# Splitting ScalarE's two-instruction pieces over two rows of the scans, in a Mamba layer with a mixture of experts

## The reference, cut to what matters

```python
xz = einsum('bld,ed->bel', h, in_proj_w);  x, z = xz[:, :1024], xz[:, 1024:]
x = silu(causal_conv4(x) + conv_b)
x_dbl = einsum('bdl,kd->blk', x, x_proj_w)        # dt_lo (32), B (16), C (16)
delta = softplus(dt_lo @ dt_proj_w.T + dt_proj_b)
for t:  hs = hs * exp(delta_t * A) + delta_t * B_t * x_t;   y_t = sum_n(hs * C_t)
y = (y + x * D) * silu(z)
x1 = layernorm(h + y @ out_proj_w.T)
# top 2 of 8 experts, softmax of the two logits
out = layernorm(x1 + sum_k w_k * (x1 @ expert_w[k].T + expert_b[k]))
```

## Time and profile before

| | |
|---|---|
| runs of the kernel | 2264.38, 2264.75 and 2259.15 us, median 2264.38 |
| the profiled execution | 2260.66 us, span 2258.9 us |
| mean granted clock of PE | 0.947 |
| busy over the span | PE 90%, DVE 88%, POOL 82%, ACT 73% |
| batches 2 to 6 | from 561.2 to 1865.3 us, 260.8 us each |

### The profile page before, as it was taken

How to read it: one execution, slowest core, us unless ns; L and a number is a source line. 1 busy time by engine, 2 the same in 40 slices (tenths; PEclk the granted TensorE clock), 3 DMA queues, 4 the chain that set the end, 5 groups by cost and what they waited for, 6 DMA issues and landing times. The chain is left out here.

```text
span 2258.9 us, 30428 instructions
## 1 busy us (share of the span) xinstructions
PE 2036.0 (90%) x8624; PEld 1200.9 (53%) x8624; DVE 1982.8 (88%) x2191; ACT 1658.4 (73%) x3074; POOL 1854.5 (82%) x1505
## 2 busy tenths in 40 slices
PE   8897779898999989999899998999899998879898
PEld 3444455455564555545555555645556455655453
DVE  5899989989999999899999999899998998989912
ACT  5767858767598866979588875988678886667534
POOL 2988999788998889889898889989898997696503
PEclk9897879989899999999999999999999999789999
DMA  5432142367754786557863678557855576495775
GB/s 164 160 108 70 40 148 77 95 212 229 246 126 124 231 289 180 137 171 233 280 172 106 209 249 264 118 153 248 293 150 136 176 245 236 146 272 189 246 270 117
DMA packets 222085, 412.79 MB, mean 183 GB/s; under 512 B 29880, under 2 KB 36152, under 8 KB 221920
## 3 DMA queue, kind: packets, MB, share of 16 engines
q1 hardware_dynamic: 180448, 322.36, 42.6%
q0 software_dynamic: 20496, 57.16, 12.4%
q10 hardware_dynamic: 20976, 31.33, 4.3%
HBM read 299.37 MB, written 85.72 MB: 170 GB/s over the span
## 5 line engine op out<-in xcount | busy, mean ns | idle before, releaser
L1784 ACT ACTIVATE dA<-delta,negA 128x512 f32<-128x512 f32 (+1 forms) x1146 | 714.4, 637 | 317.4 <-DVE hst L1976 250.1
L1925 POOL TENSOR_TENSOR hst<-u,Bbc 128x512 f32<-128x512 f32 x666 | 880.7, 1427 | 57.4 <-PE hTp L1334 36.3
L1976 DVE TENSOR_TENSOR_SCAN hst<-dA,hst 128x512 f32<-128x512 f32 x672 | 790.3, 1207 | 44.0 <-ACT dA L1784 36.8
L1334 PEld LDWEIGHTS hTp<-ident,hst 128*128 128x128 f32 x4096 | 496.2, 149 | 318.4 <-issue 172.2
L1334 PE MATMUL hTp<-ident,hst 128*128 128x128 f32 x4096 | 557.9, 288 | 96.5 <-DVE hst L1976 24.4
L1965 DVE SCALAR_TENSOR_TENSOR y<-hTp,Ct,y 128x1024 f32<-128x1024 f32 x463 | 585.1, 1264 | 54.5 <-PE hTp L1334 51.6
L1925 POOL TENSOR_TENSOR first_dbu<-u,Bbc 128x512 f32<-128x512 f32 x222 | 295.1, 1411 | 16.5 <-DVE hits L2057 11.6
L1976 DVE TENSOR_TENSOR_SCAN hst<-dA,first_dbu 128x512 f32<-128x512 f32 x224 | 263.2, 1207 | 17.7 <-issue 9.1
L1318 PE MATMUL bank<-wslot,hidT 128*128 128x512 f32 x512 | 250.3, 621 | 8.1 <-ACT zs L1666 6.2
L1318 PE MATMUL bank<-wslot,tokT 128*128 128x512 f32 x496 | 233.3, 598 | 4.0 <-ACT tokT L1686 3.9
L1318 PE MATMUL bank<-delta,tokT 128*128 128x512 f32 x480 | 224.4, 600 | 0.0
(11 more groups left out here) (187 smaller groups left out, 2886.7 us busy)
## 6 DMA issues: line engine op xcount, KB each, us to landing
wslot<-in_w_expT SPq DMA_DIRECT2D x90, 1024.0 KB
Bbc<-b_scratch SPq DMA_DIRECT2D x113, 256.0 KB
wslot<-in_w_inT SPq DMA_DIRECT2D x26, 1024.0 KB
y<-scaled POOLq DMA_DIRECT2D x49, 512.0 KB
zs<-sorted_tokens ACTq DMA_DIRECT2D x91, 256.0 KB, 6.1
sorted_results<-ysb SPq DMA_DIRECT2D x90, 256.0 KB
res<-in_w_expT SPq DMA_DIRECT2D x18, 1024.0 KB, 5.7
gate_scratch<-zs SPq DMA_DIRECT2D x64, 256.0 KB, 2.8
```

What stands on the lines that cost most here:

```text
L1334: mm = nc.tensor.transpose(hTp[q % 2][:, tok(j)], hst[n % 2][:, j, start:start + P], ident[:, :])
L1784: nc.scalar.activation(decay_of(step, halved), delta[w.odd][:, j, cols], ACT.Exp, scale=negA[:, j, n:n + 1]).then_inc(exp_done, 1)
L1925: nc.gpsimd.tensor_tensor(dbu_row(n, j), u[w.odd][:, j, :], Bbc[n % 2][:, :], ALU.mult).then_inc(dbu_done, 1)
L1976: nc.vector.tensor_tensor_scan(hst[n % 2][:, j, :], dA[j % 2][:, :], dbu_row(n, j), 0.0, ALU.mult, ALU.add).then_inc(scan_done, 1)
```

## The change

ACT's plan for batches 2 to 6 is rewritten after planning, while the other engines keep theirs. Every double piece is issued as two single ones, the second at the earliest in the next row, that is behind the next row's exponential. The order of the pieces is kept: what stood behind a double piece in the same row follows its second half into the next row. `Segment.single` then keeps `piece` from calling the second half itself. In numbers: of 149 ACT pieces in a batch 48 are doubles (8 each of z, z2, sig2, dt, dt2 and 4 each of ln1, ln2), and all 48 second halves move by one row. Along with them 18 other pieces move by one row: z2 of tiles 0, 5 and 7, x2, scale6, x6, sig and sig2 of group 5, scale7, sig and sig2 of group 7, skip 2, 4 and 6, the copies xsT2 and xsT3, dt2 of groups 2 and 4. No instruction is added or removed.

```diff
+def one_by_one(pieces, steps):
+
+    rows, last = [], 0
+    for row, x, _ in pieces:
+        for k, name in enumerate(SINGLE.get(x[0], (x[0],))):
+            last = min(max(row + k * (last <= row), last), steps - 1)
+            rows.append((last, (name,) + x[1:], 0))
+    return rows
...
         self.fine = any(x[0] in ("dt1", "rs1") for x in pieces)
+        self.single = self.fine or steps == STEPS
...
+        if self.single and not self.fine:
+            order["act"] = one_by_one(order["act"], steps)
...
                     nc.scalar.activation(a, a, ACT.Ln, bias=1.0).then_inc(sig_step, 1)
-                    if not w.seg.fine:
+                    if not w.seg.single:
                         piece(w, ("sig3", j))
```

## The result

| | before | after |
|---|---|---|
| runs | 2264.57 us median of 4 (2259.15 to 2268.25) | 2335.36 us median of 4 (2320.26 to 2340.14) |
| ratio | | 1.0303, 95% interval 1.0259 to 1.0346 |
| profiled execution | 2260.66 us, span 2258.9, clock 0.947 | 2320.26 us, span 2318.5, clock 0.936 |
| busy | PE 90%, DVE 88%, POOL 82%, ACT 73% | PE 89%, DVE 86%, POOL 80%, ACT 71% |
| batches 2 to 6 | 1304.1 us, 260.8 each | 1369.8 us, 274.0 each |

The change makes the kernel 3% slower, 7 us beyond the top of the range. The profiled execution, 2320.26 us, is the fastest of after and lies inside the range; of the others, at a granted clock of 0.928 to 0.934, only time and clock are on record.

A forecast was written before the change was run, and what follows sets the result against it. The prediction took PE and DVE, running almost without a break, to bound the kernel. Its terms summed to 9.8 us a batch, 49 us in five, giving 2310 us against the profiled 2260.66, with a range from 2273 to 2328.

The forecast's parts named there:

- (d): Rows 79 to 80: x6's copy goes behind exponential 80, sig3 and scale6, DVE's taps wait; 2.5 us a batch.
- (a): z0, row 39: exponential 40 comes ahead of z1 to z3, the yT copies come 1.25 later; 0.8 us a batch.
- (b): Rows 70 and 74: copies x0 and x2 each go behind an exponential and a third half; 0.7 us a batch.
- (c): Row 78: sig3 goes ahead of x5, behind an exponential for which ACT must idle; 0.6 us a batch.
- (f): skip3: exponential 95 comes later and dt3 goes in between, so PE's yinit3 is late; 0.9 us a batch.
- (h): moe4, dt_5 and yinit4 follow dt_4's moved halves; exponential 111 and the copies behind slip; 0.9 us a batch.
- the 0 net: Rows 46 and 53: earlier exponentials win at most 1.6 us a batch, taken as 0 net of delays behind them.
- (e): Row 82: sig7's last half is late, POOL's product and PE's xproj follow at +1.4; 1.0 us a batch.
- (g): Rows 99 to 100: copies xsT2 and xsT3 come later and PE's moe2 waits for them; 2.4 us a batch.
- rival of the clock: Row 82 and moe2: PE's clock falls more often, seven drops of 1.7 us, 12 us on top, 2322; chance 0.14.
- later waits absorb half: DVE's waits for ACT overlap with its lateness; 4.9 us a batch, 24 us, 2285; chance 0.17.
- faster: Rows 46, 53, 62, 66, 95: DVE's waits for dA go, halves stay hidden; 2.2 a batch, 2250 us; chance 0.11.

The follow-up runs named there:

- e7: The kernel before with only the eight norms a batch (ln1 and ln2) split; 2255.66 us, ratio 0.9994.
- e9: The kernel of e6 plus two extra 512-column matmuls ahead of x7 and wT's four small matmuls done twice; 2312.2 us, ratio 1.0243.
- e13: The kernel of e8, with each share of the x projection waiting for its own tile of x; ratio 1.0183.
- e14: The kernel of e9, with each share of the x projection waiting for its own tile of x; ratio 1.0177.
- e6: The kernel after, with PE turning token tile 3 seven times instead of once, right ahead of moe2; 2321.31 us, ratio 1.0273.
- e8: The kernel after, with x2, x6, scale6, scale7, skip2, skip4, skip6, xsT2 and xsT3 kept ahead of the exponential; 2309.55 us, ratio 1.023.
- e12: The kernel after, with each share of the x projection waiting for its own tile of x; ratio 1.0265.

## Why the prediction was wrong in size

The direction, the places and what starts the loss were right: halves moved behind exponentials that wait for scans, and what stands behind them is late by the exponential and the idle time. What two of the steps left out is how that lateness goes on, through POOL's line and through PE's clock. The terms against the rows:
- **(d) x6**: 2.5 foretold, 2.45 in the rows of every batch; the taps wait 2.59.
- **(a)**: 0.8 foretold, 0.8 lost at row 42. The place was another: PE did not wait 1.6 at part 40 but 1.27 ahead of it, for the moved z1 of tile 0 (L1679), which reads the bank that PE writes next. z3's wait is 0.92 (0.86 before).
- **(b), (c)**: 0.7 and 0.6 foretold; rows 70 to 74 lose 0.6 and row 78 0.4. The earlier exponentials of rows 46 and 53 gain about 1.0 each in e7, and rows 47 and 63 take back 0.7 and 0.9, much as the 0 net had it.
- **(f)**: 0.9 foretold, 0.7 measured, 0.5 of it not for skip3 but for dt1 of group 1, whose bank moe1 waits 0.52 for.
- **(h)**: 0.9 foretold for rows 107 to 127, 0.9 measured: scan 110 falls behind by 1.9 for POOL's product, 1.1 of it comes back by row 112, as foretold.
- **(e) is the first step that failed**: 1.0 foretold, 2.9 measured. It counted ACT's six instructions up to the last half of sigmoid 7, rightly (3.8 foretold, 3.7 measured), and let POOL multiply at once: +1.4, of which 1.0 was kept. POOL has an order too. Product 6, which ran at 1253.54, ahead of the end of scan 80, now waits for a half behind exponential 82, and the scatter, a scan product and product 7 follow it in line: 1291.13 - 1287.44 = 3.7 us. The product is late by 2.55, not 1.4. The prediction said that each engine waits in line behind what waits for a moved piece, and did not work this line out. The sum also left out a second path of about the same length, the low clock at the bias matmuls, which struck in four of five batches. Either path alone holds the rows (e9, e13); without both the loss is gone (e14).
- **(g) is the second**: 2.4 foretold, 4.0 measured. The copy was late by 2.4 and cost 2.3, as worked out (e6, e9, e14). But behind a wait of 3.5 us PE ran at 1.2 GHz, and the matmuls and parts behind it cost 1.7 us more in rows 98 to 100. Another 0.7 follows in rows 100 to 107 (0.84 in the kernel after, 0.13 wherever the padding kept the clock), for which the sum had nothing. This was the rival of the clock. It struck in all five batches, at 2.4 a batch and not at the 1.7 foretold for a drop. I had given it 0.14.

Too small were thus (e) by 1.9, (g) by 1.6 and rows 100 to 107 by 0.8, and the other terms together were 1.0 too large: 9.8 to 13.1 a batch, 17 us in all. The clock rival's 2322 lies near the profiled 2320.26 partly by luck: it priced seven drops on top of a full sum, and those at the bias matmuls add nothing that the padding could win back, since POOL's product was late as well. The range's own arithmetic has a slip too. The lower bound of 16 us gives 2277, not the 2290 that the prediction names as the low end of the sum.

The rule of the Trainium skill (TensorE: Matmul & The Clock Gate, Part 1) that the clock follows how busy PE was lately agrees with these traces: the padding that kept PE busy ahead of moe2 gave 1.00 where the kernel after has 0.50.

The rival "later waits absorb half" failed: waits for dA did fall at rows 46 and 53, but grew at rows 47, 63 and 95 (from 0.4, 0.2 and 1.6 us a batch to 1.1, 1.7 and 1.9), and the 15 to 20 us foretold for them were 34.2. The rival "faster" had its places right and nothing measurable in them: e7. That leaves the difference of the medians, 71 us against 60 of the profiled pair. The executions without a trace have a lower clock, which fits more of the same drops, but no row shows it, so this stays open.

## What to carry to other kernels

When a piece moves behind an instruction that waits, follow its consumer's queue and not only the piece: each in-order engine that takes it adds what stands between, and a piece also holds the buffer that it reads. Price a lengthened stop of PE twice, once for the stop and once for the matmuls behind it at half clock: at moe2 every stop of 2.96 to 3.54 us was followed by it, and none of 1.24. And where padding or an earlier wait alone gains nothing, try both before the place is called free, for two paths of equal length hide each other. Look at every batch for this, since one batch shows only the path that was longer there.

## What was not expected of the hardware

- In batch 4 of the kernel after a wait of PE of 3.54 us is followed by a part of eight 128x128 transposes in about 1.8 us (3.62 for two) instead of 1.0 (1.91 for two), and the pair of matmuls takes 2.05 instead of 1.10. In other batches and runs the pair takes 1.10 to 2.08 behind waits of 2.96 to 3.54, but always the pair or the parts are slow. After a wait of 0.92 with the padding ahead of it there was none of it.
- e8's 2.96 us of wait at the same place gave 1.84 for the pair, so 0.6 us less of waiting was no escape.
- PE's order of work is the same in e12 and e13, and it met the low clock at the bias matmuls in two of five batches in the one and in all five in the other, with ACT's pieces in another order. Which batch is hit is not settled by the waits that these rows show.
